# A second sample group on the dense path, and sums over samples by accumulated transposes on TensorE

## The reference, cut to what matters

```
v = (xn @ v_w + v_b)                       # 4 x 32 x 32 x 8 groups x 32 channels
deform = (deform(xn) + prior) * sigmoid(scale(xn) + dscale) * 6.0    # x, y of every sample
weights = (xn @ qw_w + qw_b)               # one weight per group and sample
samp = bilinear sample of v at (w + dx, h + dy): 4 corners, zero outside the image
out = sum over the 9 samples k of samp[k] * weights[k]
x = x + (out @ out_w + out_b)
```

## Time and profile before

| | |
|---|---|
| Median of 3 runs | 3019.55 us (3014.43 to 3028.98) |
| The profiled execution | 3027.92 us, span 3025.8 us |
| TensorE busy | 2254.1 us, 16544 instructions, mean granted clock 0.853 |
| VectorE busy | 2084.3 us, 4371 instructions |
| ScalarE busy | 1094.1 us |
| GpSimd busy | 2175.3 us |

### The profile page before, as it was taken

The page is one execution under the profiler, slowest core; times in us unless marked ns, Lnnn a source line. Parts: engine busy times, 40 slices in busy tenths (PEclk is TensorE's granted clock), DMA queues, the critical chain, the costliest instruction groups (busy, mean ns, idle before and its releaser), DMA issues.

```text
span 3025.8 us, 54249 instructions
## 1 busy us (share of the span) xinstructions
PE 2254.1 (74%) x16544; PEld 2134.3 (71%) x16544; DVE 2084.3 (69%) x4371; ACT 1094.1 (36%) x3526; POOL 2175.3 (72%) x2085
## 2 busy tenths in 40 slices
PE   1355667787877777887787878778787877777788
PEld 0354657777777777787777778777777777777777
DVE  4556657677767677876677777767677766777643
ACT  1012224333434343343343334334343433443355
POOL 2777777777777777777777777777777777777700
PEclk6677778898988889898888888988888988888899
DMA  9511212222212222221222222122111111111100
GB/s 185 129 53 53 60 49 61 61 61 61 60 54 54 60 61 60 62 61 54 56 61 61 61 61 60 53 55 60 57 54 54 53 55 49 54 54 54 55 15 10
DMA packets 262111, 181.03 MB, mean 60 GB/s; under 512 B 187923, under 2 KB 224805, under 8 KB 262021
## 3 DMA queue, kind: packets, MB, share of 16 engines
q0 software_dynamic: 64512, 132.25, 14.3%
q1 hardware_dynamic: 197508, 47.77, 7.5%
HBM read 157.48 MB, written 22.37 MB: 59 GB/s over the span
## 4 chain that ended last, share of the span: by engine, by line
POOL 58%; issue 21%; PE 10%; DVE 6%; SPq 3%; DMA 1%; ACT 1%; POOLq 1%; DVEq 0%; ACTq 0%
POOL got L751 57%; PE Y L1422 3%; PE Z L1413 2%; PE N L1326 1%; SPq L635 1%; DVE got L967 1%; DVE acc L1042 1%; DVE summed L970 1%; SPq L614 1%; DMA got<-patches,ranks 1%; PE N L1480 1%; PE N L1488 1%; POOL ranks L743 1%; DVE made L890 1%; ACT hid L1239 0%
## 5 line engine op out<-in xcount | busy, mean ns | idle before, releaser
L751 POOL DMA_INDIRECT got<-patches,ranks x2016 | 2152.6, 1068 | 652.5 <-issue 592.5
L1422 PE MATMUL Y<-w,hid 128*128 128x128 f32 x4096 | 653.9, 311 | 577.2 <-DVE acc L1042 492.2
L1422 PEld LDWEIGHTS Y<-w,hid 128*128 128x128 f32 x4096 | 584.6, 220 | 611.0 <-DVE acc L1042 379.1
L1239 ACT ACTIVATE hid<-Z,b 128x128 f32<-128x128 f32 x2048 | 576.6, 369 | 641.2 <-PE Z L1413 640.2
L1326 PE MATMUL N<-ident,made 128*128 128x128 f32 x4608 | 577.4, 286 | 76.7 <-issue 43.9
L1326 PEld LDWEIGHTS N<-ident,made 128*128 128x128 f32 x4608 | 557.6, 201 | 95.3 <-issue 58.8
L1413 PE MATMUL Z<-xt_m,w 128*128 128x128 f32 x4096 | 586.0, 293 | 0.5 <-ACT xt_m L1221 0.5
L1413 PEld LDWEIGHTS Z<-xt_m,w 128*128 128x128 f32 x4096 | 545.9, 208 | 13.3 <-issue 7.2
L970 DVE TENSOR_REDUCE summed<-got 128x32 f32<-128x1152 f32 x224 | 475.4, 2122 | 7.7
L967 DVE TENSOR_TENSOR got<-got,wq 128x1152 f32<-128x1152 f32 x224 | 303.0, 1353 | 159.1 <-DMA got<-patches,ranks 159.0
L890 DVE TENSOR_TENSOR made<-tent 128x1024 f32<-128x1024 f32 x288 | 341.3, 1220 | 9.6 <-PE N L1326 8.1
(11 more groups left out here) (204 smaller groups left out, 2260.8 us busy)
## 6 DMA issues: line engine op xcount, KB each, us to landing
got<-patches,ranks POOLq DMA_INDIRECT x2016, 2.4
vwin<-vpad SPq DMA_DIRECT2D x320, 40.0 KB
patches<-arena SPq DMA_DIRECT2D x92, 128.0 KB
patches<-got SPq DMA_DIRECT2D x38, 128.0 KB, 3.6
w<-in_L_ffn_w SPq DMA_DIRECT2D x2, 2048.0 KB
vpad<-vt SPq DMA_DIRECT2D x128, 16.0 KB
out<-X SPq DMA_DIRECT2D x32, 64.0 KB, 1.8
X<-in_x SPq DMA_DIRECT2D x1, 576.0 KB, 4.5
```

Source lines behind the costliest of these rows:

```text
L751: pool.indirect_dma_start(out=got[:, q, j * PATCH:(j + 1) * PATCH], out_offset=None, in_=table, in_offset=bass.IndirectOffsetOnAxis(ap=ran ...
L1239: ins = a.activation(hid[:, e % 2, c, :], Z[e % 2][:, c * P:(c + 1) * P], ACT.Relu, bias=b1[n][:, e * FC + c:e * FC + c + 1])
L1422: ins = pe.matmul(Y[:, (e % 4) * D:(e % 4 + 1) * D], hid[:, e % 2, c, :], w2[n][:, e * FC + c, :], start=(c == 0), stop=(c == FC - 1))
```

## The change

- `DG` goes from 7 to 6: two groups are dense, six are gathered. `patches`, `rank`, `wq` and the place arithmetic behind the clamp shrink to 6 groups; the tents and `make` go from 9 to 18 samples for each tile, still with three buffers `made`.
- The dense sums carry `is_transpose=True`: TensorE accumulates transposes, 9 samples in one group A, 9 in a second B, in the same banks `N`. Each is copied (`copyA`, `copyB`) and looked up (`lookA`, `lookB`); the results stand in a new bank `S`.
- The reduce L970 is gone. After the product, TensorE transposes the nine samples' blocks of `got` of a group into one 128 x 128 block of `S`, accumulated, also with `is_transpose=True`. `S` holds three groups; ScalarE copies it twice for each tile (`half0`, `half1`) into `sums`. The corners are then summed by the projection, whose weights `ow` are repeated four times: six matmuls, one for each group, and one for the dense pair, which `turn` transposes.
- GpSimd waits for TensorE's `g` of a group instead of VectorE's reduce.
- In `slots` the dense steps begin at e = 6 of the pass before and go on to e = 7; `lookB` stands at e = 0 of `beside_first`, ahead of the attention's queries; the tents move from e = 6, 7 to e = 4, 5. The sixth gathered group is the last.
- `OT` takes the memory of `PT`.

```diff
-DG = G - 1
+DG = G - 2
 NQ = DG
+HALF = NQ // 2
+GJ = DG * K
+KD = GK - GJ
...
                         if ends:
                             conv("turn", i - 1, i - 1 + PLEAD if placed else last)
+                        dense("make", i, range(4, 6))
+                        dense("sum", i, range(2, 4))
                     if e == 1:
...
-                        dense("make", i, range(0, 2))
+                        dense("make", i, range(6, 8))
+                        dense("sum", i, range(4, 6))
                     if e == 2:
...
-                        dense("sum", i, range(0, 2), i - 4 if att else None)
-                        dense("make", i, range(2, 4))
+                        dense("make", i, range(8, 10))
+                        dense("sum", i, range(6, 8))
                     if e == 3:
...
-                        dense("sum", i, range(2, 4))
-                        dense("make", i, range(4, 5))
+                        dense("make", i, range(10, 12))
+                        dense("sum", i, range(8, 9))
+                        dense("copyA", i)
...
-                        dense("sum", i, range(4, 5))
-                        dense("make", i, range(5, 7))
+                        dense("make", i, range(12, 14))
+                        dense("sum", i, range(9, 11))
+                        dense("lookA", i)
                     if e == 5:
...
-                        dense("sum", i, range(5, 7))
-                        dense("make", i, range(7, 9))
+                        dense("make", i, range(14, 16))
+                        dense("sum", i, range(11, 14))
                     if e == 6:
...
+                        dense("make", i, range(16, 18))
+                        dense("sum", i, range(14, 16))
                         conv(0, i)
-                        dense("sum", i, range(7, 9))
-                        dense("copy", i)
                     if e == 7:
...
+                        dense("sum", i, range(16, 18))
+                        dense("copyB", i)
                         conv(1, i)
-                        dense("look", i)
 
                 def beside_first(e):
                     if e == 0:
+                        dense("lookB", i)
...
                     if e == 4:
...
+                        if tents:
+                            dense("apart", i + 1)
                     if e == 5:
...
+                        if tents:
+                            dense("weigh", i + 1)
...
                         if tents:
-                            dense("apart", i + 1)
+                            dense("make", i + 1, range(0, 2))
...
-                        if not final:
-                            conv(6, i)
                         if tents:
-                            dense("weigh", i + 1)
+                            dense("make", i + 1, range(2, 4))
+                            dense("sum", i + 1, range(0, 2), i - 3 if att else None)
...
-                            pool.wait_ge(*conv_v.done(f"r{q}", t - 1))
+                            pool.wait_ge(*conv_t.done(f"g{q}", t - 1))
...
                     v.tensor_tensor(g3, g3, wj.unsqueeze(2).to_broadcast([P, QJ * CORNERS, C]), ALU.mult)\
                         .then_inc(*s(f"m{q}"))
-                    v.wait_ge(*d(f"m{q}", t))
-                    v.tensor_reduce(summed[:, q * C:(q + 1) * C],
-                                    got[:, q, :].rearrange("p (j c) -> p c j", c=C), AX.X, ALU.add)\
-                        .then_inc(*s(f"r{q}"))
...
+                if part == HALF - 1:
+                    a.wait_ge(*conv_t.done(f"g{HALF - 1}", t))
+                    a.wait_ge(*dense_t.done("lookB", t))
+                    a.wait_ge(*conv_t.done("proj", t - 1))
+                    a.activation(sums[:, 0:half_sums + DC], S[:, 0:half_sums + DC], ACT.Copy)\
+                        .then_inc(*conv_s.step("half0"))
+                if part == NQ - 1:
+                    a.wait_ge(*conv_t.done(f"g{NQ - 1}", t))
+                    a.activation(sums[:, half_sums + DC:], S[:, 0:half_sums], ACT.Copy)\
+                        .then_inc(*conv_s.step("half1"))
...
                             ins = pe.matmul(N[c // 4][:, (c % 4) * P:(c % 4 + 1) * P],
                                             made[:, k % MADE, c * P:(c + 1) * P], ident[:, :],
-                                            start=(k == 0 and c % 4 == 0), stop=(k == K - 1 and c % 4 == 3))
+                                            start=(k % K == 0 and c % 4 == 0), stop=(k % K == K - 1 and c % 4 == 3),
+                                            is_transpose=True)
...
-                        ins = pe.matmul(N[0][:, 0:C], spread[:, c, :],
-                                        v_dense[:, bass.ds(t // TB * TB + c, 1), :].rearrange("p o c -> p (o c)"),
+                        ins = pe.matmul(S[:, half_sums + n * C:half_sums + (n + 1) * C], spread[:, c, :],
+                                        v_dense[:, bass.ds(t // TB * TB + c, 1), n * C:(n + 1) * C]
+                                        .rearrange("p o c -> p (o c)"),
...
+                if isinstance(part, int):
+                    q = part
+                    pe.wait_ge(*conv_v.done(f"m{q}", t))
+                    if q % HALF == 0:
+                        pe.wait_ge(*(conv_s.done("half1", t - 1) if q == 0 else conv_s.done("half0", t)))
+                    for j in range(QJ):
+                        ins = pe.matmul(S[:, (q % HALF) * P:(q % HALF + 1) * P],
+                                        got[:, q, j * PATCH:(j + 1) * PATCH], ident[:, :],
+                                        start=(j == 0), stop=(j == QJ - 1), is_transpose=True)
+                    ins.then_inc(*s(f"g{q}"))
...
-                    pe.matmul(CV[:, 256:384], summed_T[:, 0, :], ow[:, 0, :], start=False, stop=False)
-                    pe.matmul(CV[:, 256:384], summed_T[:, 1, :], ow[:, 1, :], start=False, stop=True)\
+                    for q in range(NQ):
+                        pe.matmul(CV[:, 256:384], turned_sum(q), ow[:, q, :], start=False, stop=False)
+                    pe.matmul(CV[:, 256:384], looked_T[:, :], owd[:, :], start=False, stop=True)\
                         .then_inc(*s("proj"))
```

More of the change, by code:

```diff
@@ L225, in build @@
         sg = part(GK)
-        pp, fl, fr, fr0, tmp = (part(2 * GK) for _ in range(5))
-        wlin = part(4 * GK)
-        wyw = part(2 * GK)
+        pp = part(2 * GK)
+        fl, fr, fr0, tmp = (part(2 * GJ).rearrange("p (a j) -> p a j", a=2) for _ in range(4))
+        wlin = part(4 * GJ).rearrange("p (s a j) -> p s a j", s=2, a=2)
+        wyw = part(2 * GJ).rearrange("p (a j) -> p a j", a=2)
         pint = wyw.bitcast(I32)
@@ L233, in build, with turned_sum @@
         first_xt = got[:, 4, :].rearrange("p (t d) -> p t d", t=LEAD)
+        half_sums = HALF * P
+        looked_at = sums[:, half_sums:half_sums + P]
+        def turned_sum(q):
+            at = q * P + (DC if q >= HALF else 0)
+            return sums[:, at:at + P]
         first_vs = got[:, 1:3, :].rearrange("p q f -> p (q f)").rearrange("p (t f) -> p t f", f=VW)
@@ L271, in build @@
         place_t = Steps(sem("place_t"), "xT offs")
-        dense_v = Steps(sem("dense_v"), "apart weigh m0 m1 m2 m3 m4 m5 m6 m7 m8")
-        dense_s = Steps(sem("dense_s"), "abs tent s0 s1 out")
-        dense_t = Steps(sem("dense_t"), "k0 k1 k2 k3 k4 k5 k6 k7 k8 look")
+        ks = range(KD)
+        dense_v = Steps(sem("dense_v"), "apart weigh " + " ".join(f"m{k}" for k in ks))
+        dense_s = Steps(sem("dense_s"), "abs tent sA0 sA1 sB0 sB1")
+        dense_t = Steps(sem("dense_t"), " ".join(f"k{k}" for k in ks[:K]) + " k9 k10 lookA " +
+                        " ".join(f"k{k}" for k in ks[K + 2:]) + " lookB")
         ts = range(LEAD)
@@ L280, in build @@
         gath_g = Steps(sem("gath_g"), "c0 c1")
-        conv_v = Steps(sem("conv_v"), " ".join(f"m{q} r{q}" for q in range(NQ)) + " add")
-        conv_t = Steps(sem("conv_t"), "T proj")
-        conv_s = Steps(sem("conv_s"), "T")
+        conv_v = Steps(sem("conv_v"), " ".join(f"m{q}" for q in range(NQ)) + " add")
+        conv_t = Steps(sem("conv_t"), " ".join(f"g{q}" for q in range(NQ)) + " T proj")
+        conv_s = Steps(sem("conv_s"), "half0 half1 T")
         route_v = [Steps(sem(f"route{n}_v"), "stats aggr eps rstd xn lg max neg eqd first hot rsum pos taken "
@@ L618, in _ @@
                 (heads[:, :], c_heads), (dec[:, :], c_dec), (tri[:, :], c_tri),
-                (ow[:, :, :], out_w.rearrange("(n p) d -> p n d", p=P)),
+                *[(ow[n * C:(n + 1) * C, :, :], out_w[0:DG * C, :].rearrange("(g c) d -> c g d", c=C))
+                  for n in range(CORNERS)],
+                (owd[:, :], out_w[DG * C:G * C, :]),
                 (rows[:, 0, :], out_b.unsqueeze(0)), (rows[:, 1, :], bproj.unsqueeze(0)),
@@ L944, in _ @@
             dense("weigh", 0)
+            dense("make", 0, range(0, 4))
             v.wait_ge(const_in, CONSTS)
@@ L1110, in attend @@
```

(15 more changed lines are left out.)

119 lines of the change are left out of this document (60 added, 59 removed).

## The result

The changed kernel took 3114.31 us (median of 4 runs, 3109.22 to 3118.11), the kernel before 3020.28 beside it (4 runs): a ratio of 1.0308, 95% interval 1.0279 to 1.0337. It is slower, as forecast; 3047 was said, so the loss is 3.1% (94 us) where 0.9% (27 us) was expected. The time lies in the range and just inside the forecast's own (2977 to 3117).

A forecast was written before the change was run, and what follows sets the result against it. It took the ring of VectorE and TensorE, 86.3 of 88.3 us a tile, as the bound beside the gathers. A 363 us head, 28 tiles of 90.5 and 156 behind gave 3053 of span, 3047 us; range 2820 to 3170.

The forecast's parts named there:

- Stretch C: `beside_first` 0 to 3, between two `add_up`s: 26.2 to 26.9 us, before 22.7, with `qbd` waiting for `lookB`.
- the ring: VectorE and TensorE walking `slots`, meeting four times a tile: 90.5 us a tile, forecast range 88 to 93, before 86.3.
- What bounds the kernel: Whole kernel before: the VectorE-TensorE ring takes 86.3 of 88.3 us a tile; fewer gathers alone win 2.
- The head: First four tiles, paced by gathers: 79 us a tile instead of 88.3, 37 us won, ending at 363.
- One instruction for a transpose, at full clock: TensorE's sums: an accumulated transpose is one instruction, priced as other work; 597 instructions a tile, 66.9 us of issue.
- rival 3: TensorE's transposes lower the clock or cost two instructions: ring near 104, 3425 us; chance 0.12.
- The ring anew: One tile's four stretches between adds recounted: 23.2, 22.5, 26.2 to 26.9 and 18.6 us, sum 90.5.
- B: `beside_second` 4 to 7: 22.5 us, before 21.1, with 2.5 for half clock behind TensorE's wait.
- rival 4: Half clock behind both looks and three short TensorE waits: ring 93 to 97, at 95 3173 us; chance 0.10.
- Four reduces are gone in C and nothing fills their place: VectorE in `beside_first` 0 to 3: four reduces, 8.5 us, were the work behind which its waits lay.
- The sum: Whole kernel: 363 + 28 x 90.5 + 156 = 3053 us of span, 3047 us of time.
- rival 1: VectorE's saving of 5.7 us a tile stays: ring 82.5, 2823 us; chance 0.17.

The follow-up runs named there:

- The two-instruction kernel: The changed kernel with `is_transpose` taken off both sums, so each transpose becomes two instructions: 3783.71 us (one run).
- Padding: The changed kernel with 32, 64 or 96 one-column memsets on VectorE between its two hardware loops: 3096.73, 3101.70 and 3091.39 us.

## Why the prediction was right in direction and short in size

Two things failed, one in the sum and one missing from it. Stretch C was put at 26.2 us and measured 28.7: the step priced the query matmuls behind the wait for `qbd` at full clock, 1.8 us, and they took 3.41 at a clock of 0.63. And all tiles were priced alike, with nothing for the second hardware loop, whose six tiles took 97.3 us for the first loop's 92.15. The mechanism of C, that the reduces had been cover for its waits, was right. That the time still fell inside 2977 to 3117 is in part luck: with the ring at 92.15, near the top of the 88 to 93 that were allowed, the 31 us of the second loop were partly made up by the last two tiles and the tail, which were shorter than said.

**What bounds the kernel.** Right. The run with fewer gathers laid the ring bare at 85.3 (said: 86.3), and the trace after has GpSimd waiting for TensorE. Its new wait on `g`, priced at nothing, cost nothing: GpSimd stood 350.8 us in it, but VectorE waited for a gather only five times, the last time near 361 us.

**The head.** Right: the adds that end C in tile 3 ended at 363.6 (said: 363). So the price of 79 us for 54 gathers stands. A gather took 1.110 us in the mean (1.068 before), so the lengthening is 54 x (1.110 - 0.945) = 8.9 a tile, within the 7.7 to 11 taken. What lengthens a gather can be counted in the traces: of the 2016 before, 253 took over 1.3 us, and each of them started while VectorE ran an instruction with two input tensors (108 under L967, 70 under L890); none of the 223 that started under the reduce L970 did. After, 309 of 1728 did, 139 of them under L917 and 95 under L993.

**One instruction for a transpose, at full clock.** Right, and rival 3 did not come about: 4608 instructions at L1353 for twice the matmuls' work, 0.11 apart, and a mean clock of 0.94 from 500 to 2200 us (0.87 in the kernel before). The two-instruction kernel shows about what it would have cost, a ring of 117.2 and 3784 us; rival 3's price, 104 and 3425, was too low. The rule cited from the Trainium skill (TensorE: Matmul & The Clock Gate, Part 4: PE-mode transpose), that the full clock does not engage for transposes, does not hold in this trace: 27 instructions, nearly all transposes, ran from 1520.6 to 1523.3 at a clock of 1.00. They stood inside a stretch that was at 1.00 already (1516 to 1518), so whether transposes alone would bring the clock up, no run shows.

**The ring anew.** Where the step said 23.2, 22.5, 26.2, 18.6, the trace has 23.8, 21.7, 28.7, 18.0. Three of the four are off by 0.6 to 0.8, with both signs; C is the term that was mis-sized, by 2.5. Its own steps, counted from the adds that begin it: `qbd` began at 7.0 (said 6.0), since `lookB` came later; half of that is `down`, which stood 0.49 for ScalarE's ReLU, and ScalarE had itself been idle until `up` was done. The query matmuls took 3.41 (said 1.8), at a clock of 0.63: they stand behind the very wait for `qbd` that the step had placed, and I had priced the half clock behind such a wait in B, not here. Those 2.6 carried through and grew to 3.1: the maximum at 13.9 (11.2), the weights at 18.6 (15.5), product 4 done at 21.1 (18.0). From there on the count was 0.5 too long: offsets 4.5 after it (4.7), end 3.2 after those (3.5). So rival 4 is true in part: half clock behind one of its short waits, at a ring of 92.2, below the 93 at which it began and inside the 88 to 93 of the forecast.

**Four reduces are gone in C and nothing fills their place.** Right, and the core of the matter. Sums alone moved bring nothing (1.0032), an own buffer for `qbd` brings back 78 us, and tents moved into C's waits leave C as long as it was.

**The sum.** 3053 of span was said, 3112.6 came, 59.6 more. Head +0.6; 92.15 instead of 90.5 in the 26 tiles of the two loops, +42.9; the second loop's excess over 92.15, six times 5.15, +30.9, a cause that the prediction did not have at all; the last two tiles at 89.4 and 81.0 instead of 90.5, -10.6; the tail from tile 31's adds 151.9 instead of 156, -4.1. Padding took only 12.7 to 23.0 off the span, 17.8 with 32 memsets, since the first tile, the last tile of the first loop and the last two tiles became longer (95.4, 95.7, 89.3 and 85.3 with 32). The miss in the time is 67: the other 8 come from the step to the median, where the prediction took off 8.4 because the profiled execution of before lay so far above it; after, the two are the same (3114.41 and 3114.31).

**The other rivals.** VectorE's saving did not stay (rival 1): it became waits, 154.0 and 139.0 us at two instructions of C. The prediction had also said that with `qbd` before 4 us the ring is under 88 and the kernel faster. That did not hold by itself: with its own buffer `qbd` began at 2.0, the ring was 88.9 and the kernel 0.65% slower than before. Only together with earlier tents was it faster.

## What to carry to other kernels

Where two engines walk one written order, cut the order at the points where they meet and price each stretch by the engine that comes last there; work taken off an engine that waits in the stretch anyway gives nothing, and may be refilled with work from a stretch where that engine is last. A buffer shared by two stages is free as long as they are far apart in time: double the length of one of them, and the sharing is the first place to look. Where a change makes TensorE wait, price the matmuls behind the wait at both levels of the clock, and let rows of a like wait decide between them. Look for packets on the instruction queues inside hardware loops, and for "issue" in the waits of the engine, before explaining a slow stretch by its order.

## What the runs showed of the hardware that was not expected

- A hardware loop can load code in each turn, about five packets of 8 KB here, and VectorE then stood 0.8 to 2.1 us in "issue" at one or two places of each turn. In the changed kernel it depends on where the loop's code lies: 32 small instructions ahead of the loop ended it. It cost 3.4 to 6.8 us a tile in the kernels with two dense groups, the clock that TensorE loses in its longer wait included. By which rule a position is good or bad was not tried.
- The same packets need not cost anything: the kernel before has 29 of them in its second loop, and VectorE stands 0.75 to 0.92 us once a turn, but a tile takes 88.1 there as in the first loop. The kernel with fewer gathers is like it, 85.2 and 85.3.
- TensorE's loop can do the same: with two instructions for each transpose it had some nine packets of 16 KB a tile and stood 2.8 us a tile in "issue". No run took this away, so its price in time is not known.
- Accumulated fp32 transposes in PSUM cost TensorE one instruction each, 0.11 us apart at full clock, and the changed kernel, with 198 of them a tile, had a higher mean clock than the one before (0.94 against 0.87). The clock does not go by their number: the kernel with the reduces kept has 144 a tile and 0.84 over the same 500 to 2200 us.
- In both kernels the gathers of over 1.3 us all started under an instruction of VectorE with two input tensors, none under its reduces.
